# Second attention: where the fourth key/value tile stands among the value products on TensorE

## The reference

```python
q = (hidden_states @ Wq.T).reshape(bsz, q_len, H, HD).transpose(0, 2, 1, 3)
k = (cross_attention_states @ Wk.T).reshape(bsz, kv_len, KVH, HD).transpose(0, 2, 1, 3)
v = (cross_attention_states @ Wv.T).reshape(bsz, kv_len, KVH, HD).transpose(0, 2, 1, 3)
q = _rmsnorm(q, q_norm_w)
k = jnp.repeat(k, GROUPS, axis=1)
v = jnp.repeat(v, GROUPS, axis=1)
k = _rmsnorm(k, k_norm_w)
scores = jnp.einsum('bhqd,bhkd->bhqk', q, k) * scale
scores = scores + attention_mask[:, :, :, :kv_len]
probs = jax.nn.softmax(scores.astype(jnp.float32), axis=-1).astype(q.dtype)
out = jnp.einsum('bhqk,bhkd->bhqd', probs, v)
out = out.transpose(0, 2, 1, 3).reshape(bsz, q_len, H * HD)
return out @ Wo.T
```

## Time and profile before

| | before |
|---|---|
| median of 3 runs | 1529.99 us (1526.86 to 1531.73) |
| profiled execution, span from first to last instruction | 1530.6 us |
| profiled execution, time of its own beside the span | not given apart from the span |
| TensorE busy | 97% of the span, 10919 matmuls |
| VectorE, ScalarE, GpSimd busy | 75%, 54%, 46% |
| mean granted TensorE clock | 0.993 |
| from the first value product of the second attention (step (0, 0)) to that of the last step | 535.8 to 1476.9 us of the span |

### The profile page before, as it was taken

How to read it: one execution, slowest core, us unless ns; L and a number is a source line. 1 busy time by engine, 2 the same in 40 slices (tenths; PEclk the granted TensorE clock), 3 DMA queues, 4 the chain that set the end, 5 groups by cost and what they waited for, 6 DMA issues and landing times.

```text
span 1530.6 us, 28713 instructions
## 1 busy us (share of the span) xinstructions
PE 1490.5 (97%) x10919; PEld 874.2 (57%) x10919; DVE 1152.5 (75%) x2139; ACT 819.6 (54%) x2497; POOL 710.4 (46%) x670
## 2 busy tenths in 40 slices
PE   6999999999999899999999999999999999999998
PEld 4888645555554555556555555555565556555554
DVE  4888777778877878677777777786687677678868
ACT  5678731212222775465556655664665565556853
POOL 5668875554564453342333233333433343334553
PEclk9999999999999999999999999999999999999999
DMA  7454345442434252322221221212112112111322
GB/s 245 148 170 137 122 85 118 105 72 42 75 76 76 74 135 46 94 53 33 57 62 31 53 68 24 62 38 55 53 46 56 49 42 56 29 29 35 53 46 111
DMA packets 223642, 113.25 MB, mean 74 GB/s; under 512 B 207264, under 2 KB 207392, under 8 KB 220816
## 3 DMA queue, kind: packets, MB, share of 16 engines
q1 hardware_dynamic: 222208, 104.07, 28.0%
q10 hardware_dynamic: 1296, 7.34, 1.5%
HBM read 57.89 MB, written 4.19 MB: 41 GB/s over the span
## 4 chain that ended last, share of the span: by engine, by line
PE 57%; DVE 4%; ACT 2%; POOL 2%; DMA 1%; issue 1%; SPq 0%; DVEq 0%
PE bank L75 18%; PE bank L77 17%; PE bank L76 17%; PE bank L2451 3%; ACT a_prob L1814 1%; PE bank L2425 1%; DMA a_pT_lo<-a_p_lo 1%; POOL a_prob L1680 1%; PE bank L2426 1%; DVE x_res L2188 1%; POOL a_p_hi L1686 0%; DVE x_res L2032 0%; POOL a_prob L1688 0%; DVE a_nmx L2077 0%; DVE w L2026 0%
## 5 line engine op out<-in xcount | busy, mean ns | idle before, releaser
L1814 ACT ACTIVATE a_prob<-a_prob,a_nmx 128x64 f32<-128x64 f32 x512 | 170.2, 333 | 236.7 <-DVE a_nmx L2077 236.7
L75 PE MATMUL bank<-w,a_oT_hi 128*128 128x512 f16 x512 | 194.0, 379 | 1.5 <-DVE a_oT_lo L2101 1.4
L77 PE MATMUL bank<-w,a_oT_hi 128*128 128x512 f16 x512 | 194.0, 379 | 0.0
L76 PE MATMUL bank<-w,a_oT_lo 128*128 128x512 f16 x512 | 194.0, 379 | 0.0
L2032 DVE SCALAR_TENSOR_TENSOR x_res<-bank,a_oinv,x_res 128x512 f32<-128x512 f32 x128 | 95.8, 748 | 121.5 <-PE bank L77 121.4
L1680 POOL TENSOR_TENSOR a_prob<-a_prob,a_mask 128x512 f32<-128x512 f32 x64 | 79.9, 1270 | 209.7 <-DVE a_prob L2071 209.7
L1159 ACT CAST f_h_hi<-h 128x448 f16<-128x448 f32 x64 | 35.6, 563 | 209.6 <-DVE h L1233 209.6
L1692 POOL TENSOR_TENSOR a_krs<-a_kve,neg_half 128x4 f32<-128x4 f32 x32 | 32.5, 1014 | 244.0 <-DVE a_kve L2056 244.0
L1686 POOL TENSOR_TENSOR a_p_hi<-a_prob,a_rden 128x512 f16<-128x512 f32 x64 | 67.9, 1060 | 111.0 <-DVE a_rden L2085 111.0
L1097 POOL TENSOR_TENSOR f_h_lo<-h,f_h_hi 128x448 f16<-128x448 f32 x64 | 72.7, 1140 | 91.4 <-ACT f_h_hi L1159 91.4
L1695 POOL TENSOR_TENSOR a_qrs<-a_qve,neg_half 128x8 f32<-128x8 f32 x64 | 103.9, 1642 | 12.9 <-DVE a_qve L2046 12.9
(11 more groups left out here) (362 smaller groups left out, 4541.0 us busy)
## 6 DMA issues: line engine op xcount, KB each, us to landing
shared<-in_l_wq SPq DMA_DIRECT2D x8, 1024.0 KB, 5.1
shared<-in_l_wo SPq DMA_DIRECT2D x8, 1024.0 KB, 5.3
shared<-in_w ACTq DMA_DIRECT2D x8, 896.0 KB, 4.7
craw<-in_w SPq DMA_DIRECT2D x11, 512.0 KB, 3.8
a_wide<-in_l_ctxT SPq DMA_DIRECT2D x16, 256.0 KB, 3.9
x_res<-in_x SPq DMA_DIRECT2D x16, 256.0 KB, 4.4
shared<-in_ctx SPq DMA_DIRECT2D x16, 256.0 KB, 4.2
shared<-in_l_wkv SPq DMA_DIRECT2D x8, 512.0 KB, 3.9
```

The costliest lines, as they stand in the source:

```text
L75: pe.matmul(out, a_hi, b_hi, start=first, stop=False)
L76: pe.matmul(out, a_lo, b_hi, start=False, stop=False)
L77: return pe.matmul(out, a_hi, b_lo, start=False, stop=last)
L1814: ins = act.activation(pt, pt, ACT.Exp, bias=nmx[:, col:col + 1], accum_out=den[:, col:col + 1])
```

## The change

`attend(i, 1)` moves ahead of the fourth key/value tile in `body` of the `tensor` block, together with the first step's wait for `s_cs`. So in each of 31 steps the value products of both halves stand one behind the other and the fourth tile behind them. No instruction is added or removed, and the lists of the other four engines are the same row by row.

```diff
                 attend(i, 0, c % 2)
-                keys_values(cn, i + 1, range(3, TPC))
                 if fresh and c == 0:
                     pe.wait_ge(s_cs, 6)
                 attend(i, 1, c % 2)
+                keys_values(cn, i + 1, range(3, TPC))
                 query_squares(i + 1)
```

## The result

The changed kernel took 1531.12 us (median of 20 runs, 1528.26 to 1533.28) beside 1528.74 for the one before in the same comparison: ratio 1.0013, 95% interval 1.0007 to 1.0019. By the ratio that is 2.0 us slower (the two medians lie 2.4 apart). The interval excludes no change, and lies inside the 0.3% called "same". The profiled execution took 1532.16 us with a span of 1530.3, so some 1.9 us lie around the span. That of the kernel before must then have taken about 1532.4, more than any of its timed runs: it was a long one.

A forecast was written before the change was run, and what follows sets the result against it. TensorE, busy 1490.5 of 1530.6 us, was taken as the bound. Terms: c=0 -1.05, c=1 -0.25, c=2 +1.0, c=3 -0.3, late landings +1.0, three others -0.6, first step +1.6: +1.4, so 1531.4 us; range 1526.0 to 1535.0.

The forecast's parts named there:

- Part 1: Behind the first value product: three changes between 64 and 128 rows become one; squares start 0.21 us earlier a step.
- Part 2: First output product, held by VectorE: gain 0.21 us in c=0 steps, 0.06 in c=1 and c=3.
- Part 3: Fourth tile's later result delays the second output addition and the fourth output product; each c=2 step loses 0.17 us.
- Part 4: Second half's value products come earlier and wait for low-probability transposes landing late in some steps; +1.0 us in all.
- Part 5: First step: second half waits for a bank, no longer covered by the tile; +1.6 us, bounds 1.5 and about 2.1.
- The landing sets every step: Second half's start: late transfer in all 31 steps, 0.37 us lost each, 1543 us in all; chance 0.07.
- The faster case: Other engines have more slack than shown, so all 31 steps gain 0.21 us: 1525.1 us; chance 0.07.
- Gaps not saved: Every group of value products costs its gap wherever it stands; nothing saved, +4.6 us, 1534.6 us; chance 0.08.

The follow-up runs named there:

- the one with five changes: Changed kernel with the fourth tile and the second half's value products cut in halves and alternating: 1534.42 us, ratio 1.0034 of the kernel before.
- the control with the tile in its old place: Kernel before, with VectorE's split of the query weights moved behind the second output addition: 1529.65 us, ratio 1.0004.
- the repetition with both losses out: Changed kernel, first step in the old order and query-weight split behind the second output addition, measured again: 1526.19 us, ratio 0.9987 of the kernel before.

## Why the prediction was right

**The sum.** Forecast +1.4 us and 1531.4; measured 1531.12, and 2.0 us slower with 1.1 to 2.9 as the interval (the later comparisons give 2.1 and 0.8). That the time is met to 0.3 us is luck in part: the forecast stands on the 1529.99 of three runs, where 20 runs of the kernel before give 1528.74, so a base 1.25 us too high made up for a difference that was 1.0 us too small between medians. The steps in the profiles give +0.7, half of the forecast.

What the timed runs have beyond the steps was not found in any stretch. From the scores of (7, 3) on every profile takes 69.5 us. The start of the program, which the change doesn't touch, differs by up to 5 us from profile to profile, so scatter can hide it; but that it is scatter is not shown. The other edited kernels, all but the one with five changes (+6.2 us in the steps, +5.2 timed), read 1.1 to 2.5 us more in the timed runs than their steps say beside the 944.02 us of the kernel before, even the control with the tile in its old place (-0.6 in the steps, +0.6 timed). The two repetitions of the kernel before don't (0.0 and -0.3; -0.7 and -0.9). So this surplus doesn't depend on the tile's place alone, and its cause stays open.

*Part 1, row changes:* right. 0.107 was taken, 0.105 a change was measured with three different counts. In (5, 2) the squares stand 2.73 us behind the first product, as forecast.

*Part 2, the first output product:* right for c = 1 and c = 3 (0.06 gained in each, as forecast). For c = 0 the gain was 0.17, not 0.21. In step (6, 0), from the first value product at 1265.54:

```profile
1267.69 1.28 DVE L2101 SCALAR_TENSOR_TENSOR a_oT_lo<-bank,a_oT_hi 128x512 f16<-128x512 f32 x2
...
1269.11 0.38 PE L75 MATMUL bank<-w,a_oT_hi 128*128 128x512 f16 x1
```

VectorE finished at 3.43 and TensorE started at 3.57, 0.14 later. The term that was mis-sized is the 0.05 us from VectorE's end to TensorE's start; that was read from a step where TensorE had waited long. Here TensorE had just run through its squares. In c = 1 and c = 3 steps the distance is 0.06, and why it is 0.14 here isn't shown.

*Part 3, the late tile:* right in mechanism and size, +0.18 for +0.17. Taking the weight split out of the chain turned it into the full gain.

*Part 4, the lost cover:* right in mechanism, mis-sized in the sum. In the c = 0 steps of groups 3 to 6 it fitted by about 0.1 us, each time. In (7, 0), whose second transfer the prediction didn't look at by itself, it didn't: the transfer landed 0.84 us behind the first product in all three profiles, and the second half began at 0.89 instead of 0.67. It cost nothing, since VectorE held that step's first output product at 4.07 before and after (30.21 us a step). The late steps were charged +1.0, read from one profile; the seven steps from (1, 1) to (2, 3) cost +0.2 against a forecast of +1.1 that includes their other terms. The kernel before pays for lateness too, at the first half: (2, 3) took 30.50 in the first profile of before and 29.84 changed. That the changed kernel was spared that wait in all three profiles, while two of the first three of before had it, is seen but not explained. One profile with the new order in group 2 had it too, the repetition with both losses out (30.15).

*Part 5, the first step:* the wait and the path are right, the size is met by luck. The mean, +1.6, rests on one early rise of the clock before (35.57 us) and one late one with the change (38.12). In the order of before the first step took 35.95 to 36.10 us in seven of eight profiles, counting the kernels of the experiments; in the new order 37.05 to 37.22 in three of four. So the usual price is 1.1 us, under the lower bound of 1.5. The term that was mis-sized is the tile's 2.67 us, carried over from before: in the first profile of the changed kernel the clock rose inside the moved tile, and from its start to the squares it took 2.15 us (540.47 to 542.62). Where the clock rose later, in the third profile, it took 2.53, the squares came 1.5 us later than before, as forecast, and the output products at the lower level made the step 2.1 us longer than in the first profile of the kernel before, the upper bound.

**The rivals.** The landing sets every step: it didn't; of the 62 blocks of value products 8 were released by a transpose, and that counts the first halves. The faster case: excluded by c = 1, 2 and 3, whose terms bound as they were worked out. Gaps not saved: excluded by the 0.11 us at the joint and by the alternating order.

## What to carry to other kernels

Before moving a block back in the order of a fully busy engine, follow its result through the other engines to the buffer that the same engine asks for next, with each link's slack; here 0.60 us later at one end (2.33 to 2.93) was 0.17 lost at the other, although the order itself saved 0.21. A gain repeated in every step (6.5 us on paper) is worth only what each kind of step has room for, and a single start-up wait can take a sixth of it or more (1.1 us here, 2.1 in one profile). Before a wait loses its cover, compare the new time of need with the landings of all steps, not with the median alone.

## What was not expected of the hardware

Each change between matmuls of 64 and of 128 rows cost TensorE 0.105 us at the upper clock level, in either direction. At the lower level the surplus was 0.14 (540.89 to 541.24 against a distance of 0.213 in the first step of before).

A wait of 5.1 us ahead of the first step's value products goes with the lower clock level (1.2 GHz, a granted clock of 0.50) in the first products of all thirteen profiles. The full level was back 3.1 us behind the first product in one of them, 5.2 to 6.3 in eleven, and not yet 8.7 us behind it in one. The order with 1.58 us of added idle, therefore, cost 1.1 us in one execution and 2.1 in another. That the added idle delays the rise isn't shown: in the other three profiles that have it the clock rose 6.0 to 6.3 us behind the first product, and in the eight with the order of before it rose at 5.2 to 6.1, but for the one at 3.1.

The same transpose of low probabilities landed in 2.4 us in all later steps and in up to 4.4 in some steps of groups 1 and 2, in steps that differ from profile to profile; what holds them up wasn't tried. In the slow ones of groups 1 and 2 the first of two transfers often held SyncE's queue for longer (2.29 us in the rows above, 1.26 in the later steps), and the second was issued late for that.
